# Loading and casting the first group of weights in halves, on two queues and by two engines

## The reference

```python
x = x + (x @ W0.T + (x @ A0[label0]) @ B0.T * 0.5)
x = x + (x @ W1.T + b + (x @ A1[slot1]) @ B1[slot1] * 2)
```

## Time and profile before

| | us |
|---|---|
| median of 3 runs | 294.64 (294.36 to 294.74) |
| the profiled execution | 294.32 |
| its span, first to last instruction | 292.6 |
| TensorE busy in it | 288.8 |
| VectorE busy | 242.8 |
| ScalarE busy | 153.9 |

### The profile page before, as it was taken

How to read it: one execution, slowest core, us unless ns; L and a number is a source line. 1 busy time by engine, 2 the same in 40 slices (tenths; PEclk the granted TensorE clock), 3 DMA queues, 4 the chain that set the end, 5 groups by cost and what they waited for, 6 DMA issues and landing times.

```text
span 292.6 us, 4450 instructions
## 1 busy us (share of the span) xinstructions
PE 288.8 (99%) x1337; PEld 236.0 (81%) x1337; DVE 242.8 (83%) x368; ACT 153.9 (53%) x270; POOL 30.4 (10%) x81
## 2 busy tenths in 40 slices
PE   8999999999999999999999999999999999999996
PEld 6888888888888888878878878878878878878885
DVE  3789996999999999999996897797798698695432
ACT  3685576879257537464453463373364355355120
POOL 1718100010000501000100100100100100100000
DMA  6999420800006600093268076068068159013004
GB/s 203 323 322 325 51 37 10 137 1 2 0 0 110 98 27 1 5 148 136 46 100 217 22 130 188 18 103 220 3 108 214 16 103 237 0 36 145 0 1 146
DMA packets 100803, 29.17 MB, mean 100 GB/s; under 512 B 85548, under 2 KB 93996, under 8 KB 100788
## 3 DMA queue, kind: packets, MB, share of 16 engines
q1 hardware_dynamic: 100788, 28.99, 42.7%
HBM read 20.59 MB, written 8.39 MB: 99 GB/s over the span
## 4 chain that ended last, share of the span: by engine, by line
PE 99%; ACT 0%; DVE 0%; issue 0%
PE bank L1204 94%; PE bank L1228 3%; PE bank L1450 1%; PE bank L1416 0%; ACT b_hi L468 0%; DVE y L718 0%
## 5 line engine op out<-in xcount | busy, mean ns | idle before, releaser
L1204 PE MATMUL bank<-v_hi,lhs 128*128 128x512 f32 (+1 forms) x136 | 42.5, 377 | 0.0
L1204 PE MATMUL bank<-vt_hi,s_hi 128*128 128x512 f32 x96 | 37.3, 389 | 0.0
L1204 PE MATMUL bank<-vt_lo,s_hi 128*128 128x512 f32 x96 | 37.3, 389 | 0.0
L1204 PE MATMUL bank<-vt_hi,s_lo 128*128 128x512 f32 x96 | 37.3, 389 | 0.0
L969 DVE STREAM_TRANSPOSE xt<-raw 128x512 int32<-128x512 int32 x32 | 32.4, 1076 | 1.4 <-DMA raw<-in_x 1.4
L1204 PEld LDWEIGHTS bank<-v_hi,lhs 128*128 128x128 f32 x136 | 25.1, 188 | 4.5
L468 ACT ACTIVATE lhs<-xt 128x512 fp32r<-128x512 f32 x32 | 19.6, 626 | 13.0 <-PE bank L1204 12.7
L1204 PE MATMUL bank<-v_lo,lhs 128*128 128x512 f32 (+1 forms) x68 | 25.7, 378 | 0.0
L1204 PE MATMUL bank<-vt_hi,lhs 128*128 128x512 f32 x64 | 22.1, 406 | 0.0
L718 DVE TENSOR_TENSOR lhs<-xt,lhs 128x512 fp32r<-128x512 f32 x32 | 21.7, 686 | 0.3
L434 POOL CAST ac<-c_hi 128x128 fp32r (+1 forms) x16 | 7.2, 450 | 135.5 <-PE bank L1204 98.5
(11 more groups left out here) (167 smaller groups left out, 662.6 us busy)
## 6 DMA issues: line engine op xcount, KB each, us to landing
raw<-in_x SPq DMA_DIRECT2D x32, 256.0 KB, 4.9
out<-y SPq DMA_DIRECT2D x31, 256.0 KB, 2.7
n<-in_L_cond_W SPq DMA_DIRECT2D x16, 256.0 KB, 5.3
a<-in_L_cond_W SPq DMA_DIRECT2D x16, 256.0 KB, 5.2
a_raw<-in_L_cond_lora_A SPq DMA_DIRECT2D x8, 128.0 KB, 2.4
b_raw<-in_L_cond_lora_Bs SPq DMA_DIRECT2D x16, 64.0 KB, 2.1
e_raw<-in_L_cond_lora_Bs SPq DMA_DIRECT2D x32, 32.0 KB, 1.8
a_raw<-in_L_cond_lora_As SPq DMA_DIRECT2D x8, 64.0 KB, 2.4
```

What stands on the lines that cost most here:

```text
L1204: return nc.tensor.matmul(ps, lhsT, rhs, start=start, stop=stop, skip_group_check=more)
```

## The change

n11's tile 0 comes as two loads of two squares each, both on SyncE's queue, with a semaphore of its own for the first (`n11_half_in`). a11's tile 0 is issued by ScalarE, as its first instruction. TensorE turns squares 1 and 0 into one bank and 2 and 3 into another, so that two engines can read them side by side, and counts `half_turned` behind square 0. VectorE casts the first bank's half into `b11_hi`, ScalarE the second's, and their low parts and copies are made by halves as well. VectorE does its cast and the first low half ahead of a11's work; POOL takes over the identity of a11's tile 0. The warm-ups are 11 of 256 columns and then 8 of 128. `w1_hi_made`, `w1_lo_made` and `w1_made` end one higher in all waits behind group 0, and some semaphores are merged (`b0_steps` for three, `m72_done` for `m2_done` and `m7_done`).

```diff
@@ SyncE
             for j in range(HK):
-                load_n(n11, 0, 0, j, n11_in[j])
-                load_a(a11, 0, 0, j, a11_in[j])
+                if j == 0:
+                    for h, there in ((0, n11_half_in), (1, n11_in[0])):
+                        sp.dma_start(n11[:, 0, PAIR[h], :], w1_v[:, 0, PAIR[h], 0, 0, :]).then_inc(there, 16)
+                else:
+                    load_n(n11, 0, 0, j, n11_in[j])
+                if j > 0:
+                    load_a(a11, 0, 0, j, a11_in[j])
@@ POOL
+            pool.wait_ge(a11_in[0], 16)
+            add_eye_a(a11, 0, w0_eyed)
             pool.wait_ge(n_eyed, 1)
@@ ScalarE
+            act.dma_start(a11[:, 0, :], w0.rearrange("(b j p) (a i) -> p b j a i", b=2, p=P, a=2)[:, 0, 0, 0, :]).then_inc(
+                a11_in[0], 16)
...
-            for j in range(2):
-                b11_high(j)
-                b11_copy(j)
+            act.wait_ge(turned, 1)
+            act.wait_ge(w1_hi_made, 1)
+            copy(b11_hi[:, 0, sides[1]], FIRST_BANK[1][:, sides[1]], w1_hi_made)
+            for h in range(2):
+                act.wait_ge(w1_lo_made, h + 1)
+                copy(b11[:, 0, sides[h]], FIRST_BANK[h][:, sides[h]], w1_made)
+            b11_high(1)
+            b11_copy(1)
@@ VectorE
-            dve.wait_ge(n11_in[0], 16)
+            dve.wait_ge(n11_half_in, 16)
             tt(n11[:, 0, 0, :], n11[:, 0, 0, :], eye[:, :], ALU.add, n_eyed)
...
+            dve.wait_ge(half_turned, 1)
+            nc.vector.tensor_copy(b11_hi[:, 0, sides[0]], FIRST_BANK[0][:, sides[0]]).then_inc(w1_hi_made, 1)
+
+            def b11_first_low(h):
+                tt(b11_lo[:, 0, sides[h]], FIRST_BANK[h][:, sides[h]], b11_hi[:, 0, sides[h]].bitcast(F32),
+                   ALU.subtract, w1_lo_made)
+
             for j in range(2):
+                if j == 0:
+                    dve.wait_ge(w1_hi_made, 1)
+                    b11_first_low(0)
                 dve.wait_ge(a11_in[j], 16)
                 if j == 0:
                     a11_high(0, sides[1])
-                part = a11[:, j, P * j:P * j + P]
-                tt(part, part, eye[:, :], ALU.add, w0_eyed)
+                else:
+                    part = a11[:, j, P * j:P * j + P]
+                    tt(part, part, eye[:, :], ALU.add, w0_eyed)
                 dve.wait_ge(w0_eyed, j + 1)
                 a11_high(j, slice(0, H) if j else sides[0])
-                b11_low(j)
+                if j == 0:
+                    dve.wait_ge(w1_hi_made, 2)
+                    b11_first_low(1)
+                else:
+                    b11_low(j)
                 a11_low(j)
@@ TensorE
-            warm_up(14)
+            warm_up(11)
             pe.wait_ge(eye_steps, 2)
-            turn_b11(0)
-            warm_up(5)
+            pe.wait_ge(n11_half_in, 16)
+            for t in (1, 0, 2, 3):
+                if t == 0:
+                    pe.wait_ge(n_eyed, 1)
+                if t == 2:
+                    pe.wait_ge(n11_in[0], 16)
+                last = nc.tensor.transpose(FIRST_BANK[t // 2][:, P * t:P * t + P], n11[:, 0, t, :], eye[:, :])
+                if t == 0:
+                    last.then_inc(half_turned, 1)
+            last.then_inc(turned, 1)
+            warm_up(8, P)
             vm1_high(0)
```

More of the change, by code:

```diff
@@ L160, in two_layer_lora_kernel @@
         n11_in = [sem(f"n11_in{j}") for j in range(HK)]
+        n11_half_in = sem("n11_half_in")
         n21_in = [sem(f"n21_in{j}") for j in range(HK)]
@@ L237, in two_layer_lora_kernel @@
         TURN_BANK = [bank[n] for n in (6, 7, 4, 5, 6, 7, 4, 5, 6, 7, 4, 6, 7, 4, 6, 7)]
-        TURNED_THERE = {4: 0, 5: 1, 6: 2, 7: 3, 8: 4, 9: 5, 10: 6, 11: 8, 12: 9, 13: 10, 14: 11, 15: 12}
+        TURNED_THERE = {2: 0, 4: 0, 5: 1, 6: 2, 7: 3, 8: 4, 9: 5, 10: 6, 11: 8, 12: 9, 13: 10, 14: 11, 15: 12}
+        FIRST_BANK = [TURN_BANK[0], TURN_BANK[2]]
         Q_BANK = [bank[5], bank[6]]
@@ L319, in load_b1 @@
                     sp.dma_start(e_raw[32 * n:32 * n + R1, :], src[:, halves[HALF[n]]]).then_inc(b1_in, 16)
-            sp.wait_ge(b0_lo_made, 1)
+            sp.wait_ge(b0_steps, 3)
             load_a0(0)
@@ L516, in _ @@
             act.wait_ge(zeroed, 1)
-            act.wait_ge(b0s_made, 1)
-            copy(b0_st[:, :, 0:R0], b0_raw[:, :, :], b0_hi_made)
+            act.wait_ge(b0_steps, 1)
+            copy(b0_st[:, :, 0:R0], b0_raw[:, :, :], b0_steps)
             s3_high(0)
@@ L690, in batch @@
                 if not final:
-                    act.wait_ge(m2_done, b + 1)
+                    act.wait_ge(m72_done, 2 * b + 2)
                     a_high(b + 1, 1)
@@ L697, in batch @@
                         s_high(b + 1, 1)
-                    act.wait_ge(m7_done, b + 1)
+                    act.wait_ge(m72_done, 2 * b + 1)
                     if not first:
@@ L740, in b11_low @@
             def b11_low(j):
-                dve.wait_ge(w1_hi_made, j + 1)
+                dve.wait_ge(w1_hi_made, j + 2)
                 tt(b11_lo[:, j, :], TURN_BANK[j][:, :], b11_hi[:, j, :].bitcast(F32), ALU.subtract, w1_lo_made)
@@ L771, in b0_sum @@
                 dve.wait_ge(b0_in, 16)
-                tt(b0_raw[:, KT:12, :], b0_raw[:, 0:HK, :], b0_raw[:, HK:KT, :], ALU.add, b0s_made)
+                tt(b0_raw[:, KT:12, :], b0_raw[:, 0:HK, :], b0_raw[:, HK:KT, :], ALU.add, b0_steps)
             def b0_low():
-                dve.wait_ge(b0s_made, 1)
-                dve.wait_ge(b0_hi_made, 1)
-                tt(b0_st[:, :, 64:64 + R0], b0_raw[:, :, :], b0_st[:, :, 0:R0].bitcast(F32), ALU.subtract, b0_lo_made)
+                dve.wait_ge(b0_steps, 2)
+                tt(b0_st[:, :, 64:64 + R0], b0_raw[:, :, :], b0_st[:, :, 0:R0].bitcast(F32), ALU.subtract, b0_steps)
             def t1_sum(j):
-                dve.wait_ge(w1_made, j + 1)
+                dve.wait_ge(w1_made, j + 2)
                 tt(t1[:, j, :], TURN_BANK[T12_AT[j]][:, :], b11[:, j, :], ALU.subtract, t1_made)
@@ L784, in t3_sum @@
                 dve.wait_ge(turned, T12_AT[j] + 1)
-                dve.wait_ge(w1_made, HK + j + 1)
+                dve.wait_ge(w1_made, HK + j + 2)
                 tt(t3[:, j, :], TURN_BANK[T12_AT[j]][:, :], b22[:, j, :], ALU.subtract, t3_made)
@@ L850, in b22_low @@
             def b22_low(h):
-                dve.wait_ge(w1_hi_made, 2 * HK + h + 1)
+                dve.wait_ge(w1_hi_made, 2 * HK + h + 2)
                 dve.wait_ge(t2_made, h + 1)
@@ L1134, in z_second @@
                 def z_second():
-                    dve.wait_ge(m7_done, b + 1)
+                    dve.wait_ge(m72_done, 2 * b + 1)
                     dve.wait_ge(z_made, b + 1)
@@ L1204, in mm, with warm_up @@
                 return nc.tensor.matmul(ps, lhsT, rhs, start=start, stop=stop, skip_group_check=more)
-            def warm_up(turns):
-                ones = nc.const_aps.tensor(1.0, [P, H // 2], BF16)
+            def warm_up(turns, cols=H // 2):
+                ones = nc.const_aps.tensor(1.0, [P, cols], BF16)
                 for n in range(turns):
-                    mm(Q_BANK[0][:, sides[n % 2]], ones[:, 0:P], ones, True, True)
+                    mm(Q_BANK[0][:, cols * (n % 2):cols * (n % 2) + cols], ones[:, 0:P], ones, True, True)
             def row_tile(tile, j, m):
                 return tile[:, j, P * m:P * m + P]
-            taken = ([(w1_made, j + 1) for j in range(HK)] + [(w1_made, HK + 1), (w1_made, HK + 2)]
-                     + [(t1_made, 1), (t1_made, 2)] + [(w1_made, HK + 3), (w1_made, HK + 4)]
-                     + [(t1_made, 3), (t1_made, 4)] + [(w1_lo_made, HK + 1)])
+            taken = ([(w1_made, j + 2) for j in range(HK)] + [(w1_made, HK + 2), (w1_made, HK + 3)]
+                     + [(t1_made, 1), (t1_made, 2)] + [(w1_made, HK + 4), (w1_made, HK + 5)]
+                     + [(t1_made, 3), (t1_made, 4)] + [(w1_lo_made, HK + 2)])
             def turn(tile, j, n, eyed=0):
@@ L1264, in vm1_high @@
             def vm1_high(j):
-                pe.wait_ge(w1_hi_made, j + 1)
+                pe.wait_ge(w1_hi_made, j + 2)
                 if j > 0:
@@ L1273, in vm1_high @@
                     mm(LOW[m][:, :], row_tile(a11_hi, j, m), b11_hi[:, j, :], j == 0, False)
-                pe.wait_ge(w1_lo_made, j + 1)
+                pe.wait_ge(w1_lo_made, j + 2)
                 for m in range(HK):
@@ L1328, in _ @@
             vm1_low(3)
-            pe.wait_ge(b0_lo_made, 1)
+            pe.wait_ge(b0_steps, 3)
             pe.wait_ge(t1_made, 2)
@@ L1359, in _ @@
             for j in range(HK):
-                pe.wait_ge(w1_lo_made, HK + j + 1)
+                pe.wait_ge(w1_lo_made, HK + j + 2)
                 last = q_step(Q_BANK[0], HK + j, B21, j, False, j == HK - 1)
@@ L1363, in _ @@
             pe.wait_ge(a1_lo_made, 1)
-            pe.wait_ge(w1_made, 3 * HK)
+            pe.wait_ge(w1_made, 3 * HK + 1)
             c_first(0, A11)
@@ L1373, in _ @@
                 q_step(Q_BANK[1], j, T3, j, j == 0, False)
```

(6 more changed lines are left out.)

12 lines of the change are left out of this document (6 added, 6 removed).

## The result

The changed kernel takes 298.30 us (median of 4 runs, 298.18 to 299.02), the kernel before 294.61 us in the same job (4 runs). The ratio is 1.0131, 95% interval 1.0119 to 1.0143: 3.7 us slower. The forecast was 294.45, no change that can be measured, with a range up to 295.1. The profiled execution took 299.02, the longest of the four; its span is 297.3 where the span before was 292.6.

What follows compares the result with a forecast made beforehand. TensorE, busy 99% of the span, was taken as the bound. The first product moving from 5.53 to 5.35 gave -0.18, all other terms 0: median 294.64 to 294.46, given as 294.45, range 294.1 to 295.1.

Steps and rivals of the forecast that it cites:

- Step 1: n11's first half, 128 KB issued at 0.78, lands at 3.2 to 3.95, 3.4 taken.
- L: The time at which n11's first half has landed, taken as 3.4.
- Step 2: Landing to first product through VectorE's casts: L + 1.95, so 5.35 instead of 5.53, a gain of 0.18.
- Steps 3 and 4: a11's first tile on ScalarE's queue lands at 3.6 to 4.2, cost 0; SyncE's later issues 0 to 0.1 earlier, 0.
- Step 5: Fewer and lighter warm-ups before and behind the transposes: 0, as long as the clock rises as before.
- Step 6: Behind the first product: the shift passes on one to one, also to the product at 8.87.
- Rival D: ScalarE's table load falls behind one of two waits; first product 6.35, plus 0.8, 295.4; chance 0.08.
- Rival E: TensorE's clock rises late at the start after idling and lighter filler; plus 1.9, 296.3; chance 0.05.
- Rival B: The two loads disturb each other; half lands at 3.6 to 3.95, time 294.66 to 295.01; chance 0.20.
- C: Rival: ScalarE's load of a11 is issued only at 2.06, behind the table load; 294.9; chance 0.07.

Runs made afterwards that it cites:

- e2_sync: The changed kernel with a11's first tile issued by SyncE again, third on its queue; 295.35 us, ratio 1.0033 to the kernel before.
- e1_table: The changed kernel with one constant copied at ScalarE's start, so the table load waits for nothing; 296.38 us, ratio 1.0057 to the kernel before.
- e4_table_sync: The changed kernel with the early constant copy on ScalarE and a11's first tile on SyncE's queue; 294.93 us, ratio 1.0030 to the kernel before.
- e6_halves: The changed kernel with early constant copy, a11's first tile on SyncE and 6 fillers of 256 columns behind the transposes; 294.67 us, ratio 1.0004.
- e3_warm: The changed kernel with 16 warm-ups instead of 11 and 10 of 256 columns instead of 8 of 128; 296.49 us, ratio 1.0062.
- b3_warm: The kernel before with the changed warm-ups alone, 11 of 256 columns and 8 of 128; 296.02 us, ratio 1.0032.
- e7_table_warm: The changed kernel with early constant copy, 16 warm-ups and 5 fillers of 256 columns, a11's first tile still on ScalarE; 295.39 us, ratio 1.0020.
- Q: Suspected cause: a11's load on ScalarE's queue holds up n11's first half; out of the changed kernel (e2_sync), 295.35 us.
- T: Suspected cause: ScalarE's table load on the path to the first product; out of the changed kernel (e1_table), 296.38 us.
- C: Suspected cause, beside Q and T: the late rise of TensorE's clock; out of the changed kernel (e3_warm), 296.49 us.
- b2: The kernel before with a second wait, on VectorE's identity in n11, ahead of ScalarE's first copy; 296.12 us, ratio 1.0041.
- v1: The changed kernel with n11's tile in one load, a11 second on SyncE, 14 and 5 warm-ups, early constant copy, a11 cast before low halves; 294.91 us.
- v3: v1 without ScalarE's second wait and without the constant copy; 294.61 us, ratio 0.9998 to the kernel before.

## Why the prediction was wrong

**Step 1, the landing L, failed.** It was put at 3.2 to 3.95, 3.4 taken. L was 4.38. The lower bound was right without ScalarE's load (3.2 in e2_sync). The 3.4 rested on SyncE's load being the first at work, and it was the second: up to 3.0 its queue moved 0.01 MB and ScalarE's 0.17. The upper bound had that order, ScalarE's 256 KB ahead of the half, but not its pace: by 3.0 both queues together had moved 0.18 MB where the kernel before had moved 0.27, and by 3.8 they had moved 0.45 MB and not the 0.38 of the bound. (That the half's last byte came at about 3.8 is an estimate, from the 0.6 us between last byte and landing of the prediction's step 1.) That no row of before had two queues was said; the bound should then not have come from rows of one. The rule of the Trainium skill ("DMA: Bandwidth & Descriptors", "Issuing engines are not separate DMA queues") was on the right side, since a second issuer gave nothing, but up to 3.0 the two loads hardly interleaved, and the loss is larger than the 3.6 that the prediction drew from it: 1.2 us for the half, from 3.2 to 4.38.

**Step 2, from L to the first product, was right in its order and short by 0.3.** It was L + 1.95; in e1_table, without the table load, it is 4.44 to 6.70, 2.26. The bank cast took 0.42 and not the 0.29 of a cast from SBUF: it reads a bank, and I had priced the subtraction beside it by a bank row but not the cast. Landing to turned half took about 0.97, put at 0.88. That VectorE, and not ScalarE, is last was right, but the table load hid it in the changed kernel: in e1_table ScalarE's half copy ended at 6.37 and VectorE's cast of a11's right half at 6.55, ahead of the product at 6.70. In e4_table_sync and e6_halves VectorE is last too, but because it waited for a11. (One of the step's sums is off by 0.02: 1.20 + 0.42 - 0.08 is 1.54, not 1.56; it changes nothing.)

**Steps 3 and 4.** a11 landed at 4.1, inside 3.6 to 4.2. Right, and worth nothing, as n11 came later still. SyncE's later issues moved by 0.03, as said.

**Step 5, the warm-ups at 0, failed.** They were priced at nothing "as long as the clock rises as before", and it didn't: 1.8 us of the 3.7 came back with more filler alone (e3_warm), and the same warm-ups in the kernel before cost 1.2 in the medians (b3_warm).

**Step 6, that a shift passes on one to one, was right** as far as waits go: no new wait stands behind the first product. The product of 8.87 didn't follow by the same amount, because of the slow steps: 2.08 at the first product and 2.66 in the steps make 4.74, and the span grew by 4.7.

**Rival D (0.08, plus 0.8) happened,** at its place: the load starts at 5.88, behind VectorE's cast. The sentence of the Trainium skill ("ScalarE: Activation LUTs", "Step-by-step: what each stage is for") that the load stands right before its ACTIVATE described it; that the load of before stood 4.1 us ahead was no evidence against it, because nothing but the copy's own single wait lay between. I read a number where I should have read the order. Its price was about right: 0.8 over the 5.53 of before is 1.0 over the sum's own 5.35, and the load moved the first product by 0.91 (e1_table) and 1.07 (e3_warm against e7_table_warm). **Rival E (0.05, plus 1.9) happened too,** with 2.66 in the profiled execution and 1.8 in the medians. **Rival B (0.20) happened and went past its end,** 3.95. C did not: ScalarE's load was issued at 0.79.

The failure of the chances is a step of its own. B, D and E were given as alternatives that share one unit of probability, each with all others absent. They come from different edits, and worse, they feed each other: B and D lengthen the time in which TensorE stands still at the start, and that is what E needs. That they feed each other shows in the runs: taking Q out of the changed kernel returned 2.95 us, T 1.9 and C 1.8, together far more than 3.7. Their prices counted from the sum's own 5.35 and 294.46 (0.55 for B, 1.0 for D, 1.9 for E, 3.45 in all) would have given 297.9 against the measured 298.3. With 0.2, 0.08 and 0.05 added up as exclusive, the range left the whole slow side out.

**The sum was made against an early execution.** The profiled one of before took 294.32, 0.32 under its median. Four kernels that leave n11's whole tile first on SyncE's queue (b2, b3, v1, v3) had it land at 3.9 to 4.1 and not at 3.6. A half microsecond of spread in the first landing is larger than the 0.18 that I forecast.

## What to carry to other kernels

Ask of every edit at a kernel's start what it does to the time in which TensorE idles before its clock is up; the price there is not only the idle time but what runs behind it at half speed, and several small delays add to one large one. Rivals that come from different edits can all be true: give each a chance of its own, add their prices, and let the range hold the sum. When a second wait is put ahead of ScalarE's first ACTIVATE, look where the table load goes; and don't let a second engine issue a load at the same moment as the most urgent one.

## What the runs showed of the hardware

Two loads issued by SyncE and ScalarE within 0.07 us of each other: the engines moved 35 GB/s (SyncE's issued first) and 151 GB/s (the changed kernel) from 1.8 to 2.6, and the 128 KB of SyncE that land in 2.4 us alone took 3.9 and 3.6. Of 0.18 MB moved by 3.0 in the changed kernel 0.17 were ScalarE's. Issued 0.76 us apart, SyncE's 128 KB took 2.6.

The granted clock can fall while TensorE is busy: in one of four executions of b2_second_wait it went to 0.50 at about 7.3, after an idle stretch of 1.5 us that ended at 6.88, and stayed there for 3.4 us. At the start the steps can be those of 1.2 GHz while the granted clock reads 1.00 (the changed kernel up to about 13.4). A cast of 128x256 took 0.29 on VectorE out of SBUF and 0.42 out of a bank.
